# Expert slots dealt in units of 128 tokens: 32 pair tiles and seven single tiles in place of 39 tiles of 256 slots

## The reference

```
x = x + conv(layernorm(x)) + layernorm(x) * omega       # long convolution along the 4096 positions, per channel
h = layernorm(x) as tokens
for batch row b, position t, taken as tokens:           # ei, ew: 4096 x 2 expert indices and weights
    y[tok] += ew * ( gelu(h[tok] @ w1A[e].T @ w1B[e]) @ w2A[e].T @ w2B[e] )      # e = ei[tok, k], k = 0, 1
x = x + y
```

## Time and profile before

| | |
|---|---|
| median of 3 runs | 1131.13 us (1130.75 to 1131.34) |
| the profiled execution's own time | 1127.49 us |
| its span, first to last instruction | 1125.5 us |
| mean granted TensorE clock | 0.943 of full |
| PE, DVE, ACT, POOL busy | 82%, 72%, 70%, 53% of the span |

### The profile page before, as it was taken

How to read it: one execution, slowest core, us unless ns; L and a number is a source line. 1 busy time by engine, 2 the same in 40 slices (tenths; PEclk the granted TensorE clock), 3 DMA queues, 4 the chain that set the end, 5 groups by cost and what they waited for, 6 DMA issues and landing times. The chain is left out here.

```text
span 1125.5 us, 32814 instructions
## 1 busy us (share of the span) xinstructions
PE 917.7 (82%) x11452; PEld 756.2 (67%) x11452; DVE 815.5 (72%) x1360; ACT 784.9 (70%) x1151; POOL 591.0 (53%) x658
## 2 busy tenths in 40 slices
PE   3760788888778787999999999999988888886881
PEld 2540676767667676777777777777867777775771
DVE  7878897979779432667676766666567989796891
ACT  3872897979879544656565656565668989896890
POOL 5625985868574233656565656565565333332330
PEclk9995898989989998999999999999998999898896
DMA  9998999999999798999999888889739999899976
GB/s 315 397 401 290 258 260 213 286 215 302 303 286 318 202 267 207 274 256 293 260 272 236 227 243 218 237 225 243 183 84 268 235 223 288 224 293 300 309 171 150
DMA packets 392136, 288.01 MB, mean 256 GB/s; under 512 B 125928, under 2 KB 339592, under 8 KB 391554
## 3 DMA queue, kind: packets, MB, share of 16 engines
q1 hardware_dynamic: 346018, 211.68, 68.8%
q0 software_dynamic: 19520, 36.26, 15.7%
q10 hardware_dynamic: 26528, 39.14, 9.7%
HBM read 197.41 MB, written 100.61 MB: 265 GB/s over the span
## 5 line engine op out<-in xcount | busy, mean ns | idle before, releaser
L1495 PE MATMUL ps<-xn,wb 128*128 128x128 f32 x2048 | 277.2, 291 | 0.0
L1495 PEld LDWEIGHTS ps<-xn,wb 128*128 128x128 f32 x2048 | 252.3, 201 | 17.5 <-issue 3.0
L597 POOL TENSOR_TENSOR cen<-xb,mean 128x512 f32<-128x512 f32 x128 | 143.0, 1118 | 224.3 <-DVE state L1300 162.1
L1273 DVE TENSOR_TENSOR xn<-cen,rstd 128x1024 f32<-128x1024 f32 x128 | 174.2, 1361 | 49.9 <-POOL cen L597 36.2
L1482 PE MATMUL ps<-xn,near 128*32 128x128 f32 x2048 | 87.6, 291 | 119.2 <-DVE xn L1273 73.3
L1095 ACT ACTIVATE cen<-ps 128x1024 f32<-128x1024 f32 x118 | 117.3, 1023 | 76.4 <-PE ps L1589 57.9
L1589 PE MATMUL ps<-carry,wb 64*128 64x256 f32 x1248 | 153.7, 386 | 10.7 <-issue 7.2
L1284 DVE TENSOR_TENSOR xb<-xb,ps 128x1024 f32 (+1 forms) x128 | 152.9, 1195 | 9.5 <-PE ps L1507 9.5
L1000 ACT ACTIVATE wb<-wide 32x1024 f32<-32x1024 f32 x126 | 144.5, 1147 | 15.7 <-DMA wide<-taps_d 13.1
L1589 PEld LDWEIGHTS ps<-carry,wb 64*128 64x128 f32 x1248 | 119.7, 188 | 47.5 <-issue 32.8
L1482 PEld LDWEIGHTS ps<-xn,near 128*32 128x32 f32 x2048 | 52.5, 113 | 142.3 <-issue 69.1
(11 more groups left out here) (177 smaller groups left out, 1425.4 us busy)
## 6 DMA issues: line engine op xcount, KB each, us to landing
xb<-L_attn_x SPq DMA_DIRECT2D x160, 512.0 KB, 10.2
out<-xb SPq DMA_DIRECT2D x72, 512.0 KB, 6.5
xb<-L_attn_x ACTq DMA_DIRECT2D x128, 256.0 KB
out<-xb SPq DMA_DIRECT2D x88, 256.0 KB, 4.5
wb<-L_ffn_w_B SPq DMA_DIRECT2D x78, 256.0 KB
wide<-taps_d SPq DMA_DIRECT2D x63, 256.0 KB
dk<-decay_d SPq DMA_DIRECT2D x63, 128.0 KB
out<-y_d SPq DMA_DIRECT2D x4, 1536.0 KB, 14.4
```

The lines of the kernel that those rows point to most:

```text
L597: pool.tensor_tensor(cen[:, k, 0:QB // 2].rearrange("p b r d -> p r b d"), unit_view(pool, g, i, k)[:, :, 0:UC // 2] .rearrange("p r (b d) ...
L1273: dve.tensor_tensor(xn[:, k].rearrange("p (b d) r -> p b d r", d=2), cen[:, k].rearrange("p b r d -> p b d r"), rstd[:, g * P:(g + 1) * P] ...
L1495: ins = pe.matmul(ps[:, QB * k + b, d * P:(d + 1) * P], wb[:, h, k * QB + b, d, :], xn[:, k, 2 * b + d, :], start=(b > 0 and d == 0), stop ...
```

## The change

Slots are now dealt in units of 128. Each expert's number of units is split into pairs and possibly an odd unit; odd units go into single tiles while there are single tiles left, everything else into pair tiles, and pairs beyond the 32nd into two singles. There are always 32 pair tiles (`NP`) and seven single tiles (`NS`), so `NQ` stays 39, and the slots are 71 units rather than 78 halves. With the counts above the 32 pair tiles hold tokens, one single tile holds 22, and six single tiles are empty. The helpers `halves`, `groups`, `tok`, `grp` and `rin` give the number of halves and groups of a tile and the running counts for the semaphores.

A single tile has one gather, one statistics and one normalization, four transposes, a `rank` of the same eight matmuls (both PE column halves now compute the same 128 slots), an `up` of two groups of eight matmuls of 128 columns, two gelus of 1024 columns, a `down` of two groups of eight, one `widen` over the full 128 rows, one weighing and one scatter. The routing on DVE grows from 10 to 36 operations in its second half, each waiting for the one before. The loop over tiles has one round less, so tiles 29 to 32 are now written out. `scatter_late` has two transfers rather than four. The core of the diff:

```diff
-    NQ = (T * TK + E * (QT - 1)) // QT
-    NSC = NQ * QT // P
-    SL = NQ * QT
+    NP = T * TK // QT
+    NS = E - 1
+    NQ = NP + NS
+    NSC = 2 * NP + NS
+    SL = NSC * P
...
-        NROUTE_DVE = 23
+        NROUTE_DVE = 49
...
-            with eng.Fori(0, TT // 4 - 1) as p:
+            with eng.Fori(0, TT // 4 - 2) as p:
...
-            for q in range(TT + 1, NQ):
+            for q in range(TT - 3, NQ):
...
+        def single(q):
+
+            return isinstance(q, int) and q >= NP
+
+        def halves(q):
+
+            return 1 if single(q) else 2
+
+        def groups(q):
+
+            return 2 if single(q) else 4
+
+        def tok(q):
+
+            return NP + q if single(q) else 2 * q
+
+        def grp(q):
+
+            return 2 * NP + 2 * q if single(q) else 4 * q
+
+        def rin(q):
+
+            return 2 * NP + q if single(q) else 3 * q
...
-                if n in (1, 2, 3, 4):
-                    q, h = NQ - 2 + (n - 1) // 2, (n - 1) % 2
-                    if h == 0:
-                        for j in range(2):
-                            wait(pool, s_s[2 * (1 - q % 2) + j], 16 * ((q + 1) // 2))
-                    scatter_half(q, q % 4, h)
+                if n in (1, 2):
+                    q = NQ - 3 + n
+                    wait(pool, s_s[2 * (1 - q % 2)], 16 * ((q + 1) // 2))
...
+                if single(q):
+                    if q == NP:
+                        for h in range(2):
+                            weigh(q - 1, (m + 3) % 4, h)
+                    if q < NQ - 1:
+                        turned(q + 1)
+                    if q > NP:
+                        weigh(q - 1, (m + 3) % 4, 0)
                 if not isinstance(q, int) or ROW0 <= q + 1 < ROW0 + TT:
...
+                prefix, units, pairs, odd, odds, at, one = (small[:, n, :] for n in range(1, 8))
+                rt(dve.tensor_copy(units, smalli[:]))
+                rt(dve.tensor_scalar(smalli[:], smalli[:], 1, None, ALU.arith_shift_right))
+                rt(dve.tensor_copy(pairs, smalli[:]))
+                rt(dve.tensor_scalar(odd, pairs, -2.0, None, ALU.mult))
+                rt(dve.tensor_tensor(odd, odd, units, ALU.add))
+                rt(dve.tensor_tensor_scan(odds, ones[:, 0:E], odd, 0.0, ALU.mult, ALU.add))
+                rt(dve.tensor_tensor(at, odds, odd, ALU.subtract))
+                rt(dve.tensor_scalar(one, at, float(NS), None, ALU.is_lt))
+                rt(dve.tensor_tensor(one, one, odd, ALU.mult))
+                rt(dve.tensor_tensor(pairs, pairs, odd, ALU.add))
+                rt(dve.tensor_tensor(pairs, pairs, one, ALU.subtract))
+                ends, begin, kept, room = units, odd, odds, at
+                rt(dve.tensor_tensor_scan(ends, ones[:, 0:E], pairs, 0.0, ALU.mult, ALU.add))
...
+                rt(dve.tensor_tensor(rank_in, rank_in, over_e(begin), ALU.add))
+                rt(dve.tensor_tensor(tmp_e, rank_in, over_e(end_slot), ALU.is_ge))
+                rt(dve.tensor_scalar(alone, alone, float(P), float(NP * QT), ALU.mult, ALU.add))
+                rt(dve.tensor_tensor(alone, alone, end_slot, ALU.subtract))
+                rt(dve.tensor_tensor(tmp_e, tmp_e, over_e(alone), ALU.mult))
+                rt(dve.tensor_tensor(rank_in, rank_in, tmp_e, ALU.add))
+                for n0, n1, last in ((0, NP, ends), (NP, NQ, alone_ends)):
+                    rt(dve.tensor_tensor(t_le[:, n0:n1, :], last[0:1, :][:, None, :].to_broadcast([1, n1 - n0, E]),
+                                         t_of[:, n0:n1, :], ALU.is_le))
...
+                if single(q):
+                    for f in range(4):
+                        for h in range(2):
+                            half_rows = slice(h * RANK, (h + 1) * RANK)
+                            c = 4 * b + f
+                            ins = pe.matmul(ps[:, 2 * b + h, f * P:(f + 1) * P],
+                                            w1bs[half_rows, k, c * P:(c + 1) * P], route_a[half_rows, 0, :],
+                                            start=True, stop=True)
+                    ins.then_inc(s_up, 1)
+                    return
...
+                if single(q):
+                    for f in range(4):
+                        for h in range(2):
+                            j = 4 * h + f
+                            ins = pe.matmul(ps[h * RANK:(h + 1) * RANK, 4, 0:P],
+                                            w2as[:, h * (FC // 2) + 4 * b + f, :],
+                                            act_at(q, b)[:, j // 2, (j % 2) * P:(j % 2 + 1) * P],
+                                            start=(b == 0 and f == 0), stop=(b == 1 and f == 3),
+                                            skip_group_check=True)
+                    ins.then_inc(s_dn, 1)
+                    return
...
+                if single(q):
+                    wait(pe, s_ys, tok(q))
+                    pe.matmul(ps[:, 7, :], route_y, w2bs[:], start=True, stop=True).then_inc(s_wo, 1)
+                    return
...
+                if single(q):
+                    if q == NP:
+                        down(q, 0)
+                    if q < NQ - 1:
+                        turn(q + 1, 1 - k)
+                    if q > NP:
+                        down(q, 0)
+                    if q < NQ - 1:
+                        rank(q + 1)
+                    down(q, 1)
+                    return
```

More of the change, by code:

```diff
@@ L878, in _ @@
             up_load(5 + PIECES - YP, 1)
-            with sp.Fori((6 + PIECES - YP) // 2, (NQ - 1) // 2) as p:
+            with sp.Fori((6 + PIECES - YP) // 2, NP // 2) as p:
                 for k in range(2):
                     up_load(p * 2 + k, k)
-            up_load(NQ - 1, 0)
+            for q in range(NP, NQ):
+                up_load(q, q % 2)
             sp.wait_ge(s_a, NQ)
@@ L1084, in tile @@
                     stage_up(q + 1)
-                for b in range(4):
+                for b in range(groups(q)):
                     if b == 2 and not first:
@@ L1088, in tile @@
                             weigh(q - 1, (m + 3) % 4, h)
-                    wait(act, s_up, 4 * q + b + 1)
-                    if isinstance(q, int) and q == NQ - 1:
-                        freed = (0, -2, 1, 2)[b]
-                    else:
-                        freed = (0, -2, -1, 1)[b]
-                    wait(act, s_dn, 4 * q + freed)
+                    wait(act, s_up, grp(q) + b + 1)
+                    if not single(q):
+                        freed = (0, -2, -1, 1)[b]
+                    elif q == NP:
+                        freed = (0, -2)[b]
+                    else:
+                        freed = (-1, 0)[b]
+                    wait(act, s_dn, grp(q) + freed)
                     act.activation(act_at(q, b).rearrange("p f t -> p (f t)"),
@@ new lines, in routing @@
+                rt(dve.tensor_tensor_scan(ends, ones[:, 0:E], pairs, 0.0, ALU.mult, ALU.add))
+                rt(dve.tensor_tensor(begin, ends, pairs, ALU.subtract))
+                rt(dve.tensor_scalar(kept, ends, float(NP), None, ALU.min))
+                rt(dve.tensor_scalar(room, begin, float(NP), None, ALU.min))
+                rt(dve.tensor_tensor(kept, kept, room, ALU.subtract))
+                alone, alone_ends, end_slot = pairs, room, kept
+                rt(dve.tensor_tensor(alone, pairs, kept, ALU.subtract))
@@ L1344, in rank_in_half @@
                 dve.tensor_copy(route_a[:, 0, :], ps[:, 5, 0:P]).then_inc(s_at, 1)
-                for h in range(2):
+                for h in range(0 if single(q) else 2):
                     dve.tensor_copy(route_a[(1 - h) * RANK:(2 - h) * RANK, 1, :],
@@ L1395, in tile @@
                 if is_in(q, NQ - 1):
-                    for h in range(2):
+                    for h in range(halves(q + 1 if isinstance(q, int) else q)):
                         normal(q + 1, 1 - k, h)
@@ L1431, in _ @@
             stage(1, NK, 0)
-            for h in range(2):
-                weigh_last(h)
+            weigh_last()
             centre(1, NK, 1)
@@ L1555, in turn @@
             def turn(q, k):
-                wait(pe, s_tn, 2 * q + 2)
-                wait(pe, s_ys, 2 * (q - 1))
+                wait(pe, s_tn, tok(q) + halves(q))
+                wait(pe, s_ys, tok(min(q - 1, NP) if isinstance(q, int) else q - 1))
+                if single(q):
+                    for c in range(KC):
+                        ins = pe.transpose(ps[:, 6, c * P:(c + 1) * P], tok_x[:, k, 0, c * P:(c + 1) * P], ident[:])
+                    ins.then_inc(s_tt, 1)
+                    return
                 for c in range(KC):
@@ L1594, in down @@
             def down(q, b):
-                wait(pe, s_ge, 4 * q + b + 1)
+                wait(pe, s_ge, grp(q) + b + 1)
                 if b == 0:
```

124 lines of the change are left out of this document (67 added, 57 removed).

## The result

The changed kernel takes **1103.5 us** (median of 4 runs, 1102.8 to 1103.9) against 1130.9 for the kernel before it (4 runs, 1127.1 to 1131.3): ratio 0.9764, 95% interval 0.9742 to 0.9786. That is 27.4 us faster by the medians; forecast were 1107 and a range of 1099 to 1118. The profiled execution has a span of 1101.7 us where before it had 1125.5, 23.8 less, and its own time is 1103.9.

What follows compares the result with a forecast made beforehand. PE was taken to set the experts' stage, with transfers a close second. Gains of 21.5 (single tiles and border), 0.6 and 3, less 1 for routing, net 24.1 us: median 1131.1 becomes 1107, range 1099 to 1118.

Steps and rivals of the forecast that it cites:

- The new `up`: Single tile's `up` on PE: 32 instructions at 0.0563 us each, 1.8 us, bounds 1.3 and 4.1; a pair has 3.65.
- rival of weight loads in series: Single tiles' `up` costs 4.1 us rather than 1.8, as weight loads come one behind the other; 1117 us, chance 0.10.
- Tile 36: Single tile that PE alone sets: parts sum to 5.97 us, with hand-overs of some 0.4 taken as 6.4 us.
- Tiles 33 to 35: Single tiles still carrying rows: 6.75 us by DVE's chain plus 1.5 of slip for transfers, 8.2 each, 24.6 together.
- the rival of the clock: Granted clock falls to 1.2 GHz for all single tiles, 12.3 us each; kernel slower at 1137 us, chance 0.05.
- the prediction's own signs of being wrong: `up` keeps 0.11 us an instruction, PEclk falls below 1.00 in these tiles, or row loads land after DVE asks.
- Rows late: Tiles 33 to 35 stay as long as the transfers are now, 10.9 us each: +8.1, 1115 us; chance 0.13.
- The border: `up` of tile 38 (T) to fourth stage: `reverse2` loses its cover, ends T+7.9, then 3.3 us: T+11.2.
- Tiles 29 to 31: Three pair tiles written out rather than looped: 0.2 us each, gain 0.6, bounds 0 and 1.
- Late scatters: Two scatters fewer between POOL's first centres in the fourth stage, where DVE waited for POOL: gain 3 us, bounds 1 and 5.
- The routing: Longer routing on DVE, 8.6 us against 2.9, brings buffer 24 at most 1.9 late: loss 1 us, bounds 0 and 5.7.
- The median: Profiled execution's 1127.5 us would become 1103.4; the earlier kernel's median, 1131.1, lies 3.6 above it, so forecast 1107.

Runs made afterwards that it cites:

- the last run: Second gather behind rank, routing chain cut in two and second reversal later, all on the changed kernel: 1085.7 us, ratio 0.9891 to the kernel before on its chip.
- a third: Changed kernel with second gather behind rank and, in single tiles, DVE's copy for rank between the two groups of row statistics: 1082.9 us, ratio 0.9588.

## Why the prediction was right, and where it was not

- **The new `up`**: 0.059 us an instruction against 0.0563 taken, bounds 0.041 and 0.128. The rival of weight loads in series is out: 1.9 us for 32 instructions, not 4.1. The Trainium skill's figure for a weight load ("TensorE: Matmul & The Clock Gate", section "LDWEIGHTS (loading the stationary operand)"), 107 ns for 128 columns, is not contradicted by this: instructions come 59 ns apart, on the two halves of the rows in turn, so each half gets one every 118 ns.
- **Tile 32**: 7.75 forecast, 7.76 measured. **Tile 36**: 6.4 and 6.73. The 0.4 in it, taken as hand-overs from the 10.59 of a pair (10.59 less 10.1 is 0.5), was the hold-back of the tile ahead: without it a pair takes 10.1, the bare sum of its parts. **Tile 37**: 6.9 and 8.04, as its `turn` waited 1.1 us for `normal`, and that for POOL's `deviation` behind a scatter.
- **Tiles 33 to 35**: 24.6 forecast, 27.2 measured. The step was right in kind (the row loads slip) and mis-sized in the slip, 1.5 us a tile. It came mostly as one wait of PE, 4.49 us at the end of tile 33, and that brought what I had ruled out: "no pause of PE in a single tile is above 1 us". The clock fell for tile 34, PE was busy 8.5 us there in place of 6.5, and rose again. So the rival of the clock has its mechanism, for one tile of six, at 2.0 us. Two of the prediction's own signs of being wrong came true here, the granted clock below 1.00 (0.90 and 0.74) and row loads that land after DVE asks (3.08 us), though the total stayed in the range. Rows late at 10.9 each is out too: 10.97, 8.90, 7.29. The loads are the largest part of the excess: without them the three tiles are 4.4 us shorter (DMA share with them 1.04, 0.94 and 0.99). The chain over POOL's scatters, which the prediction didn't have, keeps them above 20.3.
- **The border**: 11.2 forecast, 11.86 measured, by the mechanism named. The reversal lost its cover and ended at T+8.8 rather than T+7.9; what follows it took 3.1 rather than 3.3. That moving it wins nothing was not seen: the next steps want it.
- **Tiles 29 to 31**: 0.6 forecast from "written out rather than looped", 3.4 measured. The step took the wrong cause. Tile 34 of before, written out but with two gathers, took 10.90, and these with one gather 10.06 and 9.62: they lose the hold-back. With the second gather moved in both kernels only 0.8 of the 3.4 is left (30.5 against 29.8): 0.43 for the smaller turn in tile 31, the rest for the loop's seam. So 2.6 us were the hold-back, and what the step named was worth some 0.4 of its 0.6.
- **Late scatters**: 3 forecast; 3.4 in the first six steps, and 4.2 (2.8 to 5.5) by the run that leaves two out. The 5.7 over the whole stage have 2.3 us of spread in them.
- **The routing**: 1 forecast, 3.3 at the end of the row statistics, 1.8 left at the first `up`. The step that failed is that a buffer that comes at 47.0 is 1.9 late and no more. While the chain ran the loads paused (share 0.71 in place of 1.05), and behind it each load was late; by the run with 26 more operations that is 2.1 us at the end of the statistics. The other 0.9 was there before the chain.
- **The median.** The sum was made against the profiled execution and 3.6 us were added for its distance to the median. The changed kernel's profiled execution lies at its median (1103.9 and 1103.5), so that offset was the luck of one run of before; without it the forecast would have been 1103.4.

Not settled: why the chip of the last run has a fast kernel before, why the kernels with the second gather moved spread over 7 to 15 us from run to run, and whether rows that start some tiles earlier, so that no single tile carries any, would give the 4 to 6 us; that was not tried.

## What to carry to other kernels

A tile of half the work does not halve its loads from elsewhere: list the bytes that ride along with a tile and compare its new length with them first. A wait of an engine for a matmul that is longer than the matmul is not cover but a question: set the waiter's start against the end of every instruction on the other engines, not only against the one that it waits for. And measure a change again once a bigger loss beside it is gone; this one was worth 27 us with the hold-back in place, and 16 to 18 without.

## What the hardware did that was not expected

- The signal of a TensorE instruction that ended while a GpSimd indirect gather ran reached DVE and ACT only some 0.5 to 0.7 us behind the gather's end, 2.2 and 2.3 us behind the start of `rank` in place of 1.1 and 1.2 (1.18 for ACT in tile 36 of before, which has no gather). In looped tiles TensorE itself broke off too and went on 0.4 us behind the gather's end. With both gathers moved `rank`'s copy comes in time (643.48 to 644.57) and `rank_out` is held in its place, until 0.36 behind the second gather (647.90 to 648.26); with the second alone moved neither is (657.98 to 659.07). That the gather causes it is shown by moving it; what in the chip holds the signal and TensorE is not. On one chip it may be absent; there is no trace of the kernel before for it.
- Behind a pause of PE of 4.49 us the tile ran at the lower clock level (3.79 us for 32 instructions that take 2.06). Behind one of 2.42 us in the same place of another kernel it did not (its `up` took 2.06), but behind one of 3.25 us in a third it did (clock 0.50 from 774.3 to 777.7), and in its tile before, with one of 2.08, too (0.51 from 764.0 to 767.4). The length of the one pause does not tell whether the clock falls.
